# Mamba stage: GpSimd's products with B in steps of two pairs, and GpSimd's products with C on 12 other pairs in place of 10

## The reference

```
dt, Bm, Cm = split(xi @ xp_w)          # after in_proj, conv, silu
dt  = softplus(dt @ dtp_w + dtp_b)
dA  = exp(dt[..., None] * -exp(A_log)) # one factor per channel and state
dBu = dt[..., None] * Bm[:, :, None, :] * xi[..., None]
h   = dA * h + dBu                     # along the sequence, per channel and state
y   = sum over states of h * C, + xi * D, times silu(z), then out_proj
```

## Time and profile before

| what | value |
|---|---|
| median of 3 runs | 6536.99 us (6535.96 to 6545.96) |
| profiled execution: time, span | 6535.6 us, 6533.6 us |
| busy over the span | PE 92%, DVE 75%, ACT 60%, POOL 67% |
| Mamba's bodies | 36, from about 2058 to 5897 us |
| granted TensorE clock | 0.991 of full, on average |

### The profile page before, as it was taken

The page is one execution under the profiler, slowest core; times in us unless marked ns, Lnnn a source line. Parts: engine busy times, 40 slices in busy tenths (PEclk is TensorE's granted clock), DMA queues, the critical chain, the costliest instruction groups (busy, mean ns, idle before and its releaser), DMA issues. The chain is left out here.

```text
span 6533.6 us, 60970 instructions
## 1 busy us (share of the span) xinstructions
PE 5998.8 (92%) x20614; PEld 2475.1 (38%) x20614; DVE 4919.0 (75%) x5709; ACT 3898.4 (60%) x6906; POOL 4396.5 (67%) x2048
## 2 busy tenths in 40 slices
PE   9999999998998888889888889888889888888898
PEld 4555555544443333323333223333223333223444
DVE  4444445544223999999999999999999999995623
ACT  4444444532225767777777777777777777774532
POOL 3333334323104999999999999999999999992300
PEclk9999999999999999999999999999999999999998
DMA  2000000122102333242323343333333232432000
GB/s 81 1 1 1 1 1 1 55 52 65 65 0 53 91 69 91 66 108 69 93 68 92 72 102 82 78 86 76 87 87 94 66 91 66 106 72 55 4 0 26
DMA packets 228680, 387.65 MB, mean 59 GB/s; under 512 B 46304, under 2 KB 64416, under 8 KB 225936
## 3 DMA queue, kind: packets, MB, share of 16 engines
q1 hardware_dynamic: 228368, 383.75, 24.1%
HBM read 207.14 MB, written 23.40 MB: 35 GB/s over the span
## 5 line engine op out<-in xcount | busy, mean ns | idle before, releaser
L2518 POOL TENSOR_TENSOR work<-work,weights 128x1024 f32<-128x1024 f32 x1152 | 2686.8, 2364 | 0.0
L2441 DVE TENSOR_TENSOR_SCAN banks<-banks,work 128x512 f32<-128x512 f32 x1584 | 1984.8, 1271 | 37.5 <-ACT banks L2486 36.9
L2395 PE MATMUL banks<-work 128*64 128x512 f32 x4608 | 1238.4, 618 | 317.4 <-POOL work L2523 277.6
L2486 ACT ACTIVATE banks<-work 128x512 f32<-128x512 f32 x2304 | 1503.2, 680 | 25.5
L1993 PE MATMUL banks<-work,weights 128*128 128x512 f32 (+31 forms) x3824 | 1221.3, 457 | 65.3 <-ACT work L2218 60.0
L2245 DVE TENSOR_TENSOR work<-banks,weights 128x512 f32<-128x512 f32 x1584 | 1055.5, 668 | 0.0
L603 POOL TENSOR_TENSOR work<-work 128x1024 f32<-128x1024 f32 x256 | 479.8, 1894 | 742.3 <-DVE work L470 741.9
L2523 POOL TENSOR_TENSOR work<-work,weights 128x1024 f32<-128x1024 f32 x360 | 848.3, 2356 | 142.0 <-ACT work L2131 141.4
L2441 DVE TENSOR_TENSOR_SCAN work<-banks,work 128x512 f32<-128x512 f32 x720 | 910.2, 1268 | 39.2 <-ACT banks L2486 39.2
L1993 PEld LDWEIGHTS banks<-work,weights 128*128 128x128 f32 x3824 | 630.8, 190 | 772.2 <-issue 571.4
L2135 ACT ACTIVATE work<-banks 128x2 f32<-128x2 f32 x792 | 136.5, 172 | 995.1 <-DVE work L2245 992.4
(11 more groups left out here) (307 smaller groups left out, 6893.9 us busy)
## 6 DMA issues: line engine op xcount, KB each, us to landing
weights<-mamba_bc SPq DMA_DIRECT2D x592, 256.0 KB, 4.9
work<-work SPq DMA_DIRECT2D x1160, 128.0 KB, 2.3
weights<-mamba_taps SPq DMA_DIRECT2D x5, 2048.0 KB, 7.6
weights<-cross_vo SPq DMA_DIRECT2D x16, 512.0 KB, 6.9
mamba_taps<-work SPq DMA_DIRECT2D x4, 2048.0 KB, 6.5
cross_vo<-weights SPq DMA_DIRECT2D x6, 1024.0 KB, 8.1
work<-in_conv_rows SPq DMA_DIRECT2D x16, 256.0 KB, 7.0
out_T<-X SPq DMA_DIRECT2D x8, 512.0 KB, 3.3
```

The source lines that it names most:

```text
L2395: mm = e.matmul(ybank[k % 2][64 * h:64 * h + 64, :], fold, ring_pair(n, j)[:, h, :], start=False, stop=(a == SP_ - 1))
L2441: e.tensor_tensor_scan(ub if by_pool(j) else da, da, ub, state[:, i:i + 1], ALU.mult, ALU.add).then_inc(scanned, 1)
L2486: e.activation(banks[:, slot_of(i), :], dt_rep[:, k % 2, h, :], ACT.Exp, scale=decay[:, f:f + 1]).then_inc(da_full, 1)
L2518: e.tensor_tensor(ring_pair(n, j), u_rep[:, k % 2], bc[:, a, 0, :].unsqueeze(1).to_broadcast([P, 2, TC]), ALU.mult) \
```

## The change

Two things change on GpSimd. The products with B are made for two pairs in one instruction over 128 x 2048 elements, which waits once and raises `fed` by 2. Its wait is now for `val(N, 32, j + 2)` with j even, so pair j-5 must have been folded. The products with C then stand behind it, for q = j-3 and q = j-2. And the table of GpSimd's pairs changes from 0, 5, 8, 11, 14, 16, 20, 24, 26, 28 to 0, 3, 5, 8, 11, 14, 16, 18, 20, 23, 24, 28, which takes two pairs (four multiplications) off VectorE. The second half of `times_x` moves from j = 31 to j = 30, behind the same products.

```diff
-BY_POOL = ((0, 5), (0, 3, 6), (0, 4), (0, 2, 4))
+BY_POOL = ((0, 3, 5), (0, 3, 6), (0, 2, 4, 7), (0, 4))
...
-                    for j in range(PAIRS_N):
+                    for j in range(0, PAIRS_N, 2):
                         k, a = j // SP_, j % SP_
                         if k == 0:
                             e.wait_ge(bc_ready[a // 2], val(N, 64, 64))
                         if a == 0:
                             e.wait_ge(rep_in[k % 2], rep_at(N, k))
-                        e.wait_ge(summed, val(N, PAIRS_N, j + 1))
-                        e.tensor_tensor(ring_pair(n, j), u_rep[:, k % 2], bc[:, a, 0, :].unsqueeze(1).to_broadcast([P, 2, TC]), ALU.mult) \
-                            .then_inc(fed, 1)
-                        q = j - BEHIND
-                        if q >= 0 and by_pool(q):
-                            e.wait_ge(kept, prod_q_at(N, q))
-                            e.tensor_tensor(ring_pair(n, q), ring_pair(n, q), bc[:, q % SP_, 1, :].unsqueeze(1).to_broadcast([P, 2, TC]), ALU.mult) \
-                                .then_inc(prod_q, 1)
+                        e.wait_ge(summed, val(N, PAIRS_N, j + 2))
+                        r = (n * PAIRS_N + j) % RING
+                        e.tensor_tensor(ring[:, r:r + 2], u_rep[:, k % 2].unsqueeze(1).to_broadcast([P, 2, 2, TC]),
+                                        bc[:, a:a + 2, 0, :].unsqueeze(2).to_broadcast([P, 2, 2, TC]), ALU.mult).then_inc(fed, 2)
+                        for q in (j - BEHIND, j + 1 - BEHIND):
+                            if q >= 0 and by_pool(q):
+                                e.wait_ge(kept, prod_q_at(N, q))
+                                e.tensor_tensor(ring_pair(n, q), ring_pair(n, q), bc[:, q % SP_, 1, :].unsqueeze(1).to_broadcast([P, 2, TC]), ALU.mult) \
+                                    .then_inc(prod_q, 1)
                         for pair in range(2):
-                            if j == (26, 31)[pair]:
+                            if j == (26, 30)[pair]:
                                 times_x(e, N, pair, x[:, (n + 1) % 2], c + 1)
```

## The result

The changed kernel takes 6779.1 us (median, 6773.2 to 6787.0), beside 6539.5 us for the kernel before in the same runs: a ratio of 1.0366 [1.0351, 1.0381]. The direction is as forecast. The size is not: the loss is 240 us where 132 were forecast, and the time lies above the range.

A forecast was written before the change was run, and what follows sets the result against it. GpSimd was to replace VectorE as the bound: 105.0 us of work plus 5.2 us of stalls make a body of 110.2 us, 3.7 more than 106.5, so 6537 + 36 x 3.7 = 6669 us; range 6595 to 6755 us.

The forecast's parts named there:

- The price of the double product: GpSimd's product with B over two pairs: 4.50 us from start to start, expected 4.40 to 4.64, saving 0.14 us each.
- The rival that hung on 3.7 us: Double product on GpSimd as cheap as 3.7 us, so VectorE sets the end at 6452 us; chance 0.10.
- GpSimd's work: Products and `times_x` on GpSimd: 105.0 us a body, was 102.6, making GpSimd the longest engine, 0.8 us over VectorE.
- The old wait goes away: GpSimd's wait for VectorE's scans, 3.8 us a body, vanishes since VectorE runs close behind the feed.
- The new waits: GpSimd stalls for TensorE's folds at products over 8, 10, 14, 16 and 18: 5.2 us a body.
- The hand-over: From the end of TensorE's fold to GpSimd's waiting product: 0.04 us, taken from ScalarE's start behind a matmul.
- Pair 23 costs nothing, hidden by C(24) and `times_x`: On GpSimd behind C(23): 4.9 us of following work hides the fold; without one part, 1.2 us more.
- VectorE's idle time: VectorE's idle time behind GpSimd's feed grows to 7 us a body.
- The loads cost nothing: SP's loads of B and C need 12.6 to 13.4 us of 13.9 available, so they cost nothing.
- the waits don't bite: Rival: folds always there in time, GpSimd's body 105.0 us and the kernel 6482 us; chance 0.06.

The follow-up runs named there:

- e12: The changed kernel with the products with B over pairs 8-9, 10-11, 14-15, 16-17 and 18-19 made singly with the old wait: 6592.6 us.
- e7: The changed kernel with 8 slots in the ring in place of 6, buffers moved to make room: 6566.1 us (control, the kernel before with 8 slots: 6551.6 us).
- e3: The changed kernel with 12 even pairs for GpSimd (0, 4, 6, 8, 10, 14, 16, 18, 20, 22, 24, 28): 6640.0 us.
- e9: The changed kernel with fillers, two zero-weight matmuls that add nothing to y, ahead of each of TensorE's folds 3, 5, 11 and 23: 6699.4 us.
- e5: The changed kernel with fillers, two zero-weight matmuls that add nothing to y, ahead of each of TensorE's folds 3, 11 and 23: 6726.7 us.
- e10: The changed kernel with 8 ring slots and 11 pairs for GpSimd, pair 3 going back to VectorE: 6612.7 us.
- e6: The changed kernel with GpSimd's product with C of an odd pair j-3 put ahead of the double product over j, j+1: 6736.9 us.

## Why the prediction was right in direction and too small

Step by step, by the parts of the prediction.

- **The price of the double product** was right: 4.53 us, and 9.04 us for two in a row, so 4.50 from start to start, from 1.08 us for each 512 columns. The Trainium skill (GPSIMD Engine Reference, section 3.1) has a measured 4497 ns for a `tensor_tensor` add of 2048 columns. The 4531 ns of the multiplication here agree within 1%. The rate of about 2.6 cycles an element in the same section of the Trainium skill, from which the prediction worked out its estimate of 4.58 us, is a little high here. The rival that hung on 3.7 us is out.
- **GpSimd's work**, 105.0 us, and GpSimd as the engine that sets the body: right; it waits for hardly anything but TensorE's folds, most of which wait for its own C, VectorE waits 320 us for its feed, and taking the fold waits away gives back 187 to 213 us (e12, e7).
- **The old wait goes away**: right for this kernel, 134.3 to 1.4 us. The reason given was "since VectorE now runs close behind the feed"; e7 shows that it was the stalls that kept it away. Once they are lifted in the same order of products, the wait for the scans is back with 1.8 us in a body (4.0 in e3, where C also stands closer behind its feed).
- **The new waits**: the mechanism and the five places (8, 10, 14, 16, a little at 18) were right, product 30 was missing, and e7 and e12 show that the waits carry the loss. **This is the step that failed, by the size of its term: 5.2 us forecast, 8.0 measured.** The 2.8 us more are 2.8 x 36 = 101 us of the 110 that the forecast is short of the median. It took the fold at 1.08 us and TensorE's steps at the pace of the earlier trace rows, all of them at the full clock, and did not ask how long TensorE would stand ahead of fold 3 when C(3) comes behind a double product. It stood 3.75 us, the longest before was 2.1; the clock went to 0.50, the fold to 1.98 us and the steps behind it to nearly twice their length. By the table in the section on the result the 2.8 us are mostly 0.8 at product 30, 0.7 at 18, 0.6 at 8, 0.45 at 16 and 0.2 at 26. With the clock kept up (e9) the stalls are 5.15 us in the body shown; in the mean they are 5.8, since there the clock still falls in some bodies.
- **The hand-over** from a fold to GpSimd was taken as 0.04 us, as ScalarE's. In e9 C(3) ends at 2305.61, the fold lasts from 2305.67 to 2306.75, and the product starts at 2306.93: 0.18 us. This is 0.14 us too little at each of four places (the end of a matmul is modelled in these profiles, so the 0.04 and the 0.18 are rough). It was in part offset by product 14, 1.22 us where 1.4 were forecast, and by product 18, where 0.2 us were forecast and none came in that body.
- **Pair 23 costs nothing, hidden by C(24) and `times_x`**: right for fold 23 itself, since the product over 28, 29, which needs it, stalls in no body. It is wrong for what comes behind: TensorE stands 3.3 us ahead of fold 23 and can come back at the lower clock, and product 30, which needs fold 25, waits 0.80 us in the mean and 1.6 to 1.9 us in 14 of the 36 bodies. With the filler ahead of fold 23 (e5, e9) product 30 waits in no body. So pair 23 costs 0.80 us a body, some 29 us in all.
- **VectorE's idle time** was forecast as 7 us in a body; it is 320 / 36 = 8.9, larger with the body.
- **The loads cost nothing**: right, 0.9 us in all, though they now land after 6.7 us in the median and not 4.9, each the median of all 592 (the loads of the earlier trace rows had 4.8); why is not known.

What the rivals were worth: the stalls do bite (e7 against the changed kernel, 213 us), and "the waits don't bite" has in e7 nearly the kernel that it describes, 6566 us where it said 6482. That rival, like my expectations of e3, e7 and e10, took GpSimd's work alone as the body, and the runs show why that is not reached: with the fold waits gone, GpSimd waits for the scans and VectorE for the feed, in one and the same body.

Three things stay open. The e9 kernel is 30 us over the forecast. About 18 us of it are the longer waits at product 10, in the bodies where the clock still falls (1.78 us in the mean in place of 1.29); how much of them the filler at fold 5 makes itself was not separated, and the other 12 us are not traced. For e7 and e10 the trace shows where VectorE stands still, at pair 28; that moving `times_x`, or making the product over 28, 29 singly, would give this back was not tested. And e7 was not run with fillers, so what the clock still costs in it, if anything, is not known.

## What to carry to other kernels

When an edit merges two instructions that wait on a ring, write down for each consumer which slot the merged wait asks for, and look for the chain "A produces, B consumes, A's next instruction waits for B": every such place costs B's full latency, here on the engine that had least to spare. Price that latency at the speed the other engine will have then, not at the speed it has in the trace of before; an engine that is made to wait longer may come back slower, and what is late can then be a step or two further on. And of two engines that feed each other, freeing one from a wait gave back less than the wait in each of these runs (e3, e6, e7, e10), since the other's wait came in its place; count the longest stretch without a feed for each of them. Last, look at all bodies and not at one: the body shown here has nearly nothing of the stall at product 30.

## What the runs showed of the hardware

- TensorE's clock falls in the middle of a stage in which it is some 88% busy. Behind a wait of 3.75 us the granted clock was 0.50, and a fold took 1.98 in place of 1.08 us. With that wait filled by two matmuls it fell two folds later, behind a wait of 2.24 us, to 0.72 in a stretch of 5 us; with that filled too it stayed at 1.00 in that body, and fell to 0.66 in another of the same run, behind a wait of 2.04 us. Matmuls without any use made the kernel 80 us faster.
- The same wait does not always have the same effect. Ahead of fold 23 of the changed kernel TensorE waited 3.31 us in one body and came back at 0.50; in another it waited 3.07 us, the clock stayed at 1.00 (3620 to 3630 us), the fold lasted 1.08 us and no stall followed.
- The mean clock says little about the cost: e7 has 0.969, no wait of GpSimd for a fold, and is 14.5 us over its control; the changed kernel has 0.963 and loses at least 80 us by it.
- GpSimd's multiplication of f32 grows evenly up to 2048 columns: 1.27, 2.35 and 4.53 us for 512, 1024 and 2048, so merging two of 1024 saves only 0.14 us.
